# Perceiver layer on one core: first block's rows by a one-hot product, output bias per block on ScalarE, and another form of the context sums and reciprocals

## The reference

```
q = layernorm(x) @ Wq + bq        # 16 heads of 32
k = ctx @ Wk + bk
v = ctx @ Wv + bv
x = x + (softmax(q k^T / sqrt(32)) @ v) @ Wo + bo
n = layernorm(x)
logits = n @ router_w + router_b  # 8 experts, the best 2 of each row are kept
gate = softmax over the kept 2
x = x + sum over experts e of gate_e * (relu(n @ w1[e] + b1[e]) @ w2[e] + b2[e])
```

## Time and profile before

| | |
|---|---|
| Runs | 1180.57, 1180.32, 1184.05 us; median 1180.57 |
| Profiled execution | 1183.44 us, of which the span of the trace is 1181.7 |
| PE busy | 1127.9 us (95%), mean granted clock 0.979 |
| DVE busy | 984.8 us (83%) |
| ACT busy | 725.7 us (61%) |
| POOL busy | 495.2 us (42%) |
| Chain that ended last | PE 89%, DVE 4%, ACT 4% |
| Attention with projections | to about 754 us of the span |
| Steps 4 to 7 of the last batch, output projection | 754 to 803 |
| Layernorm, router, table, block 0's rows | 803 to 833 |
| Expert blocks | 833 to the end, 37.0 us each |

### The profile page before, as it was taken

One profiled execution on the slowest core, in us unless ns is written; L12 is line 12 of the kernel. 1 busy time (PEld: TensorE's weight loads), 2 busy tenths in 40 slices (PEclk: granted clock), 3 DMA queues, 4 the chain that ended last, 5 costly groups with the idle time before them and its releaser, 6 DMA issues.

```text
span 1181.7 us, 24893 instructions
## 1 busy us (share of the span) xinstructions
PE 1127.9 (95%) x8016; PEld 1077.0 (91%) x8016; DVE 984.8 (83%) x2290; ACT 725.7 (61%) x1499; POOL 495.2 (42%) x429
## 2 busy tenths in 40 slices
PE   4899999999999999999999999877999999999996
PEld 3799999999999999999999999865899999999996
DVE  6568888888888989889888888877888888888886
ACT  3455656656566565655656565633577777777774
POOL 5366555556647556565655654320011111111111
PEclk9899999999999999999999999996899999999999
DMA  5231212212122121211212120312777877778874
GB/s 184 80 94 42 64 54 60 63 52 60 43 72 60 43 72 40 63 50 62 63 49 63 43 60 24 118 46 99 244 243 236 269 238 236 234 246 270 237 234 116
DMA packets 81644, 136.74 MB, mean 116 GB/s; under 512 B 11529, under 2 KB 36233, under 8 KB 81617
## 3 DMA queue, kind: packets, MB, share of 16 engines
q1 hardware_dynamic: 78496, 129.12, 34.3%
q0 software_dynamic: 3120, 7.28, 2.9%
HBM read 130.29 MB, written 6.09 MB: 115 GB/s over the span
## 4 chain that ended last, share of the span: by engine, by line
PE 89%; DVE 4%; ACT 4%; issue 1%; DMA 1%; DVEq 1%; POOL 0%; ACTq 0%; SPq 0%; POOLq 0%
PE ps L1530 16%; PE ps L414 13%; PE ps L416 12%; PE ps L415 12%; PE ps L1385 8%; PE ps L1439 7%; PE ps L1531 6%; PE ps L1423 5%; PE ps L1424 4%; PE ps L1523 1%; ACT y_gated L875 1%; PE ps L1397 1%; PE ps L1566 1%; DMA wq_raw<-in_wq_dram 1%; ACT w_hi L799 1%
## 5 line engine op out<-in xcount | busy, mean ns | idle before, releaser
L555 POOL TENSOR_TENSOR ctx_hi<-ctx_raw,no_query 128x1152 fp32r<-128x1152 f32 x64 | 142.4, 2225 | 292.3 <-PE ps L416 282.8
L963 DVE SCALAR_TENSOR_TENSOR k_mix<-ps,bk_sb,k_mix 64x384 fp32r<-64x384 f32 (+1 forms) x256 | 162.3, 634 | 82.2 <-ACT k_mix L716 78.0
L756 ACT ACTIVATE probs<-ps,negmax 128x1152 f32<-128x1152 f32 x64 | 78.3, 1223 | 198.4 <-DVE negmax L1045 198.4
L414 PE MATMUL ps<-wv_hi,ctx_hi 128*128 128x256 f32 (+1 forms) x624 | 181.8, 291 | 6.6 <-DVE k_mix L963 6.4
L559 POOL TENSOR_TENSOR ctx_lo<-ctx_raw,ctx_hi 128x1152 fp32r<-128x1152 f32 x64 | 179.6, 2807 | 5.0
L416 PE MATMUL ps<-wv_hi,ctx_lo 128*128 128x256 f32 (+1 forms) x624 | 175.7, 282 | 0.0
L415 PE MATMUL ps<-wv_lo,ctx_hi 128*128 128x256 f32 (+1 forms) x624 | 174.9, 280 | 0.0
L1530 PE MATMUL ps<-xg_mix,w_hi 128*128 128x320 f32 x584 | 165.7, 351 | 0.6 <-DVE h_sum L1223 0.6
L716 ACT ACTIVATE k_mix<-ps,bk_sb 64x384 fp32r<-64x384 f32 (+1 forms) x256 | 150.8, 589 | 25.2 <-PE ps L416 20.8
L1530 PE MATMUL ps<-h_mix,w_hi 128*128 128x320 f32 x576 | 161.4, 349 | 2.8 <-DVE h_mix L1229 1.9
L1058 DVE TENSOR_TENSOR pt_mix<-ps,pt_mix 128x384 fp32r<-128x384 f32 (+1 forms) x256 | 142.3, 580 | 2.8 <-ACT pt_mix L767 2.8
(11 more groups left out here) (203 smaller groups left out, 2707.1 us busy)
## 6 DMA issues: line engine op xcount, KB each, us to landing
w_raw<-in_w_dram SPq DMA_DIRECT2D x76, 1024.0 KB, 5.6
ctx_raw<-in_ctx_t_dram SPq DMA_DIRECT2D x48, 576.0 KB, 3.8
ctx_raw<-in_ctx_t_dram SPq DMA_DIRECT2D x16, 673.5 KB, 4.1
q_both<-q_scratch SPq DMA_DIRECT2D x14, 128.0 KB, 3.2
x<-in_x_dram SPq DMA_DIRECT2D x1, 1024.0 KB, 5.5
wq_raw<-in_wq_dram SPq DMA_DIRECT2D x1, 1024.0 KB, 7.8
q_scratch<-q_out SPq DMA_DIRECT2D x1, 1024.0 KB, 5.6
wo_raw<-in_wo_dram SPq DMA_DIRECT2D x1, 1024.0 KB, 5.4
```

The source lines that it names most:

```text
L414: pe.matmul(acc_ap, a_hi, b_hi, start=start, stop=False)
L555: nc.gpsimd.tensor_tensor(ctx_hi[slot][:, :, 0:n], ctx_raw[slot][:, :, 0:n], no_query[:].rearrange("p (o i) -> p o i", o=1).broadcast_to([ ...
L963: last = nc.vector.scalar_tensor_tensor(out=k_mix[other, 2 * a + i, cols], in0=ps[rows, bank, 0:m], scalar=bk_sb[rows, a:a + 1], in1=k_mix ...
```

## The change

It has three parts.

1. **Context sums and reciprocals.** In 7 of 8 steps `take_context` makes one reduction (lower half, into `pv_low`), an addition of PV's first piece and `pv_low`, and two additions with PV's second piece; the bank is given back after the last of them, where it was after the reductions. The reciprocal is written straight into `rinv_all`, by two reciprocals of 64 partitions, and the operation that placed it goes. POOL's bias and splits after the attention are cut into 4 pieces each.
2. **First block's rows.** The normalised rows are split (`xn_hi` on ACT, `xn_lo` on DVE, two halves each), and block 0's rows come as the product of these with `sel`: 32 matmuls of 160 columns. The finding of its token numbers moves behind its first two hidden tiles. Its indirect fetch goes.
3. **Output bias.** The product of gates and b2, its transposes and DVE's additions to `acc` go. b2 is turned into columns, the block's expert's column is copied to `b2_cur`, and ACT adds it to the second piece of the output (`part_outputs`), in a tile `yt_part` that DVE then adds to the first piece. The output's start is stored from `acc` as soon as the layernorm is through.

```diff
-                    nc.gpsimd.memset(head_of[h * HALF:(h + 1) * HALF, h:h + 1], 1.0).then_inc(tables_ready, 1)
...
-            nc.gpsimd.tensor_tensor(wo_lo[:], wo_raw[:], wo_hi[:].bitcast(F32), ALU.subtract).then_inc(wo_split, 1)
+            for k in range(KD):
+                nc.gpsimd.tensor_tensor(wo_lo[:, k, :], wo_raw[:, k, :], wo_hi[:, k, :].bitcast(F32),
+                                        ALU.subtract).then_inc(wo_split, 1)
...
-            gather_rows(0)
-            pool.wait_ge(y_summed, TT)
-            nc.gpsimd.dma_start(out_rows, acc[:]).then_inc(sums_stored, 16)
+            pool.wait_ge(xn_ready, 2 * TT)
+            for half in range(2):
+                tiles = slice(half * TT // 2, (half + 1) * TT // 2)
+                nc.gpsimd.dma_start(out_rows[:, tiles, :], acc[:, tiles, :]).then_inc(rows_moved, 16)
...
+            def rows_high(half):
+                tiles = slice(half * TT // 2, (half + 1) * TT // 2)
+                act.wait_ge(xn_ready, TT + (half + 1) * TT // 2)
+                nc.scalar.copy(xn_hi[:, tiles, :], xn[:, tiles, :]).then_inc(xn_high, 1)
...
             warm(ACT.Exp, 3)
+            rows_high(0)
             turned_high(1)
+            rows_high(1)
...
+            def part_outputs(b):
+                act.wait_ge(gate_set, b + 1)
+                for m in range(KD):
+                    act.wait_ge(y_product, KD * b + m + 1)
+                    nc.scalar.activation(yt_part[:, m, :], ps[:, m, BLOCK:2 * BLOCK], ACT.Identity,
+                                         bias=b2_cur[:, 0, m:m + 1]).then_inc(y_parted, 1)
...
+                if s < STEPS - 1:
+                    parts = 2 * ((STEPS - 1) * b + s)
+                    nc.vector.tensor_reduce(pv_low[:], ps[HALF:P, PV_BANK, 0:2 * P].rearrange("p (i r) -> p r i", i=2),
+                                            AX.X, ALU.add).then_inc(pv_part, 1)
+                    dve.wait_ge(pv_part, parts + 1)
+                    nc.vector.tensor_tensor(pv_high[:], ps[0:HALF, PV_BANK, 0:P], pv_low[:], ALU.add).then_inc(pv_part, 1)
+                    dve.wait_ge(pv_part, parts + 2)
+                    for h in range(2):
+                        rows, cols = slice(HD * h, HD * (h + 1)), slice(NQ * h, NQ * (h + 1))
+                        to = HALF * (s % 2) + HD * h
+                        last = nc.vector.tensor_tensor(ot_raw[to:to + HD, s // 2, tokens_of(b)],
+                                                       ps[rows, PV_BANK, P + NQ * h:P + NQ * (h + 1)],
+                                                       pv_high[rows, cols], ALU.add)
+                    last.then_inc(pv_free, 1)
+                    return
...
                         dve.wait_ge(total_ready, n + 1)
-                        nc.vector.reciprocal(rinv[:], total[:]).then_inc(rinv_ready, 1)
-                    if c == 1:
-                        dve.wait_ge(rinv_ready, n + 1)
-                        nc.vector.tensor_scalar(rinv_all[:, :, s], head_of[:], rinv[:, 0:1], None,
-                                                ALU.mult).then_inc(diag_ready, 1)
+                        for h in range(2):
+                            rows = slice(h * HALF, (h + 1) * HALF)
+                            part = nc.vector.reciprocal(rinv_all[rows, h, s:s + 1], total[rows, :])
+                        part.then_inc(diag_ready, 1)
...
-                nc.vector.tensor_copy(idx_cur[:], idx_next[:])
+                nc.vector.tensor_copy(b2_cur[:], b2_cols[:, expert, :])
+                nc.vector.tensor_copy(idx_cur[:], idx_next[:])
...
-                    dve.wait_ge(y_product, KD * b + m + 1)
-                    nc.vector.tensor_reduce(yt[:, m, :], ps[:, m, 0:2 * BLOCK].rearrange("p (i s) -> p s i", i=2),
-                                            AX.X, ALU.add).then_inc(y_summed, 1)
+                    dve.wait_ge(y_parted, KD * b + m + 1)
+                    nc.vector.tensor_tensor(yt[:, m, :], ps[:, m, 0:BLOCK], yt_part[:, m, :], ALU.add).then_inc(y_summed, 1)
...
-            dve.wait_ge(gates_turned, 1)
-            nc.vector.tensor_copy(gates_t[:], ps[0:E, 3, :]).then_inc(gates_t_ready, 1)
-            w1_low_piece(0, 1)
+            for piece in range(PIECES):
+                w1_low_piece(0, piece)
...
-            for t in range(TT):
-                dve.wait_ge(b2_product, t + 1)
-                nc.vector.tensor_tensor(acc[:, t, :], ps[:, t, :], acc[:, t, :], ALU.add).then_inc(y_summed, 1)
...
             with dve.Fori(0, blocks) as b:
+                expert = dve.value_load(table[0:1, bass.ds(b, 1)], min_val=0, max_val=E - 1)
...
-            find_rows(0)
-            pe.wait_ge(gates_t_ready, 1)
-            for t in range(TT):
-                pe.matmul(ps[:, t, :], gates_t[:, t * P:(t + 1) * P], b2_sb[:], start=True,
-                          stop=True).then_inc(b2_product, 1)
-            turn_rows(0, 32)
+            pe.wait_ge(sel_ready, 1)
+            pe.wait_ge(xn_split, 2)
+            for half in range(2):
+                for k in range(2):
+                    d = slice((2 * half + k) * P, (2 * half + k + 1) * P)
+                    for t in range(TT):
+                        to = ps[:, 4 + half, k * BLOCK:(k + 1) * BLOCK]
+                        pe.matmul(to, xn_hi[:, t, d], sel[:, t, :], start=(t == 0), stop=False)
+                        last = pe.matmul(to, xn_lo[:, t, d], sel[:, t, :], start=False, stop=(t == TT - 1))
+                last.then_inc(xg_turned, 1)
             for c in range(HIDDEN_AHEAD):
                 hidden(0, c)
+            find_rows(0)
```

98 lines of the change are left out of this document (53 added, 45 removed).

## The result

The kernel before takes 1181.63 us (median of 4 runs, 1180.32 to 1184.05), the change 1194.70 us (median of 4, 1193.35 to 1196.76). The ratio is 1.0105, with a 95% interval of 1.0089 to 1.0122: **slower by 1.1%**, some 13 us. I had predicted 1177.8 us with a range up to 1181.5, so the result lies outside it on the other side of the old time. The profiled execution of the change took 1194.05 us (span 1192.3, mean granted clock 0.981), 10.61 more than the 1183.44 of the profiled execution before.

The account below looks back on a forecast made before the run. In the attention an 11.05 us loop through DVE and ACT was taken to set the pace, PE having 0.33 less. Terms 5.2 - 4.5 - 4.4 + 0.9 = -2.8 took 1180.57 to 1177.8 us, range 1169.0 to 1181.5.

Parts of the forecast that it names:

- Context sums: Steady attention steps: the new chain of additions costs nothing, covered by DVE's wait for ACT.
- The rival in which DVE's freed time reaches PE: Attention: shorter additions shorten the loop every step and PE's waits go, -6.6; 1166.0 us in all, chance 0.05.
- Reciprocals, +5.2: Attention: two reciprocals hold each other and the next piece, 0.32 against 0.19 us a step; +5.2 us (-2.0 to +10).
- my 40 steps: Attention: the number of steps in which the reciprocals' 0.13 us was taken to count.
- The rival in which they overlap: Attention: the reciprocals overlap, so it gives 2.0 us instead of costing 5.2; 1170.6 us in all, chance 0.22.
- the slower one: Attention: changing partition halves costs two drains of 0.27, 0.35 us more a step, 14.0 in all; 1186.6 us, chance 0.07.
- Last steps, -4.5: Last batch's end: additions undisturbed by POOL save 3.4 us, PE's higher clock 1.1; -4.5 us (-2.5 to -5.5).
- Block 0, -4.4: Way to block 0's first hidden tile: 32 matmuls let PE start it earlier; -4.4 us (-2.5 to -5.4).
- The rival in which block 0 gives its gain back: Block 0: first tiles wait for DVE's weight pieces anyway, 3 of 4.4 us lost; 1180.6 us in all, chance 0.15.
- Loop, +0.9: Start of each block: one more number loaded on DVE costs 0.1 us (0 to 0.3), over 9 blocks +0.9.
- ACT's share of the output's sum: Block's end: ACT's part of the output sum fits its idle time and costs nothing; without that, 0.4 us a block.

Follow-up runs that it names:

- e6: The kernel before with the change's context sums alone; 1178.09 us, ratio 0.9967.
- e7: The kernel before with the change's two reciprocals alone; 1186.58 us, ratio 1.0040.
- e8: The change with one load a block (b2's column carried) and block 0's rows from high pieces only, 16 matmuls for 32; 1183.46 us, ratio 1.0002.
- e19: The kernel before with an unused second load at each block's start and 16 POOL memsets ahead of both adding DMAs; 1189.64 us, one run.
- e1: The change with one number loaded a block, the next expert's b2 column being carried in b2_next; 1182.28 us, ratio 0.9999.
- e9: The change with its second load moved from the block's start to behind the eighth hidden tile; 1180.26 us, ratio 0.9989.
- e11: The kernel before with an unused second load behind the first weight piece of a block; 1182.51 us, ratio 1.0002.
- e16: The kernel before with an unused load behind the second weight piece of a pass; 1182.58 us, one run.
- e17: The kernel before with three unused loads in a row mid-pass, behind the tenth hidden tile's weight piece; 1180.48 us, one run.
- e2: The kernel before with a second, unused load on DVE at each block's start; 1193.19 us, ratio 1.0095.
- e3: The kernel before with two unused loads on DVE at each block's start, three loads in all; 1197.76 us, ratio 1.0126.
- e15: The kernel before with an unused load as the last thing of a pass, ahead of the jump back; 1194.15 us, one run.
- e18: The kernel before with an unused second load at each block's start and 16 POOL memsets between the two adding DMAs; 1193.72 us, one run.

## Why the prediction was wrong, point by point

- **Context sums, costed at nothing in the steady steps: right.** The additions became as short as I said, and DVE waits longer for ACT (1.67 us in the step that is shown). The rival in which DVE's freed time reaches PE fell: in e6 PE's steps are what they were.
- **Reciprocals, +5.2: the mechanism right, the size a fifth too small.** The second reciprocal and the piece behind it are held: 0.35 in place of 0.19, where I had 0.32. With my 40 steps that is 6.4 us, and 6.4 is what the attention became longer. That the table shows +5.3, almost my number, is luck: this execution of the change began its attention 1.1 us earlier. e7's +4.6 is what remains of 6.6 at the end of the kernel. The rule of the Trainium skill ("VectorE: DVE Perf Modes", section "Two Vector instructions with no wait between them") was the right one of the two sides, and this trace bears it out for operations of one column in SBUF, with 0.16 a step. The rival in which they overlap fell, and the slower one, 0.35 a step more, as well; its drains of 0.27 no run shows.
- **Last steps, -4.5: the mechanism right, the clock wrong.** The steps gave 5.0, against a trace of before that was at the upper end of the spread of the old attention (33.6 to 36.0). That the clock "should then be at the upper level" was true for 773 to 776, but the lower level that follows the idle time behind 788 now lasted 10 us and not 3, and met more of PE's work: 2.4 us lost again. In my sum the clock appeared only as a gain.
- **Block 0, -4.4: 3.8 of it came, and 1.2 went again.** A matmul of 160 columns took 0.22 and not 0.15 at the lower clock, close to my upper bound (7.4 for 32 of them; it was about 6.9), with DVE's table, as e8 shows, no earlier. I let DVE's low pieces follow the table at once; ACT's load of its number and its high piece stand between (0.8 and 0.4). Then block 0 took 1.2 longer from its first hidden tile to its turned outputs. The finding of the token numbers, which I had moved into it at no cost, holds 0.94 us of its chain, and the clock reaches the full level about 840 and not 838, though the block starts 1.8 earlier; how the 1.2 divides no run shows. The rival in which block 0 gives its gain back described this, but by another wait.
- **Loop, +0.9: here the prediction failed.** The step read: "Today the first operation of a pass starts 0.34 after one of 0.33, so the branch and one load cost the overlap, 0.1; for another I take 0.1 (0 to 0.3), and 9 blocks make **+0.9**." Measured are 1.44 us a block, 11.5 in eight, and 12.4 or 14.4 us by the medians (12.1 or 11.4 by the traces) when the load is taken out or moved. The 0.34 was not the price of a load, it was what a load leaves visible behind 1.2 us of work that DVE's engine had in its queue. One load with its register work took 0.32 + 0.19 in the sequencer, which the chain of the kernel before shows at each block (L1298), and I priced the second by what remained of the first. With that row the term would have been at least 0.5 a block, and 0.7 as e19 has it for a plain second load, and the sum +1 to +3 in place of -2.8: at the upper end of my range or above it, though not yet the 13 us. The other half, 0.7 us more in the company of the adding DMA, none of my rows showed; the trace of before held one long load, PE's 1.08 us beside POOL's store (L1578).
- ACT's share of the output's sum, costed at nothing: right (e1).
- My slower rival had the wrong mechanism. The right one, a wait on a sequencer rather than on an engine, was not among the cases, although one of the few instructions that the change adds to the loop of the blocks is of this kind.

Put together: 5.3 - 5.0 + 2.5 - 0.9 - 3.8 + 1.2 is -0.7 at the end of block 0, and 11.5 more in the loop make 10.8, against 10.6 by the profiled executions.

## What to carry to other kernels

In this kernel a load of a number, which the sequencer handles alone, cost nothing while its engine had work queued (e9, e11, e16, e17), and its whole time, 0.7 us and more, when it had not (e2, e19): the first load of a loop's pass hides behind the last operations of the pass before, the second does not. Price it from the sequencer's rows and not from the gap that is visible, and put it where a long operation runs (here that was worth 11 to 14 us, with the same instructions). Half a microsecond on the busiest engine at the start of each pass counts once a pass; and when PE's idle time moves, look for the work that the lower clock will meet next. And where two traces are compared stretch by stretch, measure from a common event and not from the start of the span: 1.1 us of start made a term look right that was 6.4.

## What the runs showed of the hardware that I had not expected

- A load of a number from an SBUF table into a register of DVE takes 0.30 to 0.33 us in the loop, and 0.19 for the register work behind it. The same load takes 0.9 to 1.1 us if it starts 2.15 to 2.55 us after POOL issued an indirect DMA that adds 128 rows to DRAM (after, e2, e3, e11, e15, e18), and 0.30 when that DMA is moved (e19) or when it starts 3.5 us after it (e3). The last of the three loads of e17 starts 2.5 us after the issue of the first fetching indirect DMA and takes 0.30, so fetching rows does not do it.
- Not every longer load has this cause: the first load of each engine, ahead of the loop, takes 0.46 to 0.56 us in every trace (DVE's L1294: 0.555), apart from PE's beside the store.
- The Trainium skill ("DMA: Bandwidth & Descriptors", section "Latency and other measured facts") gives a `tensor_load` a floor of about 600 ns. Here the load's own row was as short as 0.299 us (e17), while loads in a row started 0.61 to 0.63 apart with their register work; which of the two the floor means the page does not say.
- The idle time ahead of the block's first operation is put down to "issue" (1.41 us); only the sequencer's own rows name the load.
